# The first microseconds of a graph kernel: whole-float32 hop 0, an earlier input wait, split biases, and weights laid out in 2 KB runs

## What is computed

```python
Xw = X @ Wv + bv
sj, si = Xw @ aw[:d, 0], Xw @ aw[d:, 0]
e = leaky_relu(sj[:, None, :] + si[:, :, None] + ab[0], 0.2)
alpha = A * exp(e)
T = alpha / (sum(alpha, axis=-1, keepdims=True) + 1e-12)
H, Xk = 0, X
for k in range(3):                  # hops 0, 1, 2
    H = H + Xk @ Wk[k] + bk[k]
    Xk = einsum('bij,bjd->bid', T, Xk)
x = layernorm(x + relu(H))
x = layernorm(x + (adj @ x) @ w)
```

## Time and profile before

| | us |
|---|---|
| median of 3 executions | 272.84 (272.76 to 273.21) |
| the profiled execution | 273.95 |
| its span | 272.1 |
| TensorE busy | 266.3 (98%) |
| VectorE busy | 216.8 (80%) |
| ScalarE busy | 191.6 (70%) |
| GpSimd busy | 190.3 (70%) |

### The profile page before, as it was taken

One profiled execution on the slowest core, in us unless ns is written; L12 is line 12 of the kernel. 1 busy time (PEld: TensorE's weight loads), 2 busy tenths in 40 slices (PEclk: granted clock), 3 DMA queues, 4 the chain that ended last, 5 costly groups with the idle time before them and its releaser, 6 DMA issues.

```text
span 272.1 us, 6029 instructions
## 1 busy us (share of the span) xinstructions
PE 266.3 (98%) x1887; PEld 246.6 (91%) x1887; DVE 216.8 (80%) x615; ACT 191.6 (70%) x437; POOL 190.3 (70%) x412
## 2 busy tenths in 40 slices
PE   8999999999999999999999999999999999999992
PEld 3899999999999999999999999999999999999991
DVE  0677788888898888889888888988888888788994
ACT  2688677776667777666777766677766677767874
POOL 2567547788777777877778787777887777657533
PEclk9999999999999999999999999999999999999998
DMA  7858245749584378545764448844883347922214
GB/s 222 292 164 135 30 147 125 81 139 150 150 151 145 58 136 140 165 142 155 126 86 123 146 155 143 150 121 79 133 161 99 117 115 87 135 75 77 79 41 154
DMA packets 28758, 34.91 MB, mean 128 GB/s; under 512 B 7091, under 2 KB 16694, under 8 KB 28726
## 3 DMA queue, kind: packets, MB, share of 16 engines
q1 hardware_dynamic: 28016, 34.12, 56.7%
q10 hardware_dynamic: 710, 0.40, 0.5%
HBM read 26.09 MB, written 8.42 MB: 127 GB/s over the span
## 4 chain that ended last, share of the span: by engine, by line
PE 93%; DVE 2%; DMA 1%; POOL 1%; ACT 1%; issue 1%; POOLq 0%; ACTq 0%
PE ps_v L1123 30%; PE ps_y L1123 16%; PE ps_out L1123 14%; PE ps_h L1123 11%; PE ps_agg L1300 10%; PE ps_v L1233 3%; PE ps_v L1237 3%; PE ps_v L1235 3%; PE ps_agg L1123 2%; DMA WY_sb<-Wk_dram 1%; PE ps_y L1151 1%; PE ps_v L1151 1%; POOL rstd L1025 1%; DVE stats L865 0%; DVE y L878 0%
## 5 line engine op out<-in xcount | busy, mean ns | idle before, releaser
L1123 PE MATMUL ps_v<-WX_hi,XT_hi 128*128 128x512 f32 (+1 forms) x128 | 47.7, 373 | 0.0
L1123 PE MATMUL ps_v<-WX_lo,XT_hi 128*128 128x512 f32 (+1 forms) x128 | 47.4, 371 | 0.0
L1123 PE MATMUL ps_v<-WX_hi,XT_lo 128*128 128x512 f32 (+1 forms) x128 | 47.4, 371 | 0.0
L1040 POOL TENSOR_TENSOR XT_lo<-xt,XT_hi 128x512 fp32r<-128x512 f32 x32 | 41.3, 1293 | 5.4 <-DVE WX_lo L964 2.7
L1052 POOL TENSOR_TENSOR alpha<-exps,adjs 128x256 f32<-128x256 f32 x31 | 22.9, 740 | 30.3 <-ACT exps L477 30.0
L1056 POOL TENSOR_TENSOR alpha_lo<-alpha,alpha_hi 128x256 fp32r<-128x256 f32 x31 | 22.8, 734 | 18.4 <-ACT alpha_hi L486 18.4
L509 ACT ACTIVATE y<-res,offset,rstd 128x256 f32<-128x256 f32 x62 | 33.6, 590 | 0.8 <-POOL offset L1016 0.8
L1123 PE MATMUL ps_y<-WY_hi,XT_hi 128*128 128x258 f32 x112 | 34.1, 304 | 0.0
L1300 PEld LDWEIGHTS ps_agg<-adjs,y 128*128 128x128 f32 x248 | 32.0, 191 | 2.3
L1300 PE MATMUL ps_agg<-adjs,y 128*128 128x128 f32 x248 | 32.7, 275 | 0.0
L502 ACT ACTIVATE V_hi<-ps_v 128x512 fp32r<-128x512 f32 x32 | 19.1, 597 | 19.1 <-PE ps_v L1123 18.9
(11 more groups left out here) (177 smaller groups left out, 838.7 us busy)
## 6 DMA issues: line engine op xcount, KB each, us to landing
xt<-xt_dram SPq DMA_DIRECT2D x32, 256.0 KB, 5.3
nodes<-nodes_dram SPq DMA_DIRECT2D x32, 256.0 KB, 5.4
out_dram<-out_sb SPq DMA_DIRECT2D x30, 256.0 KB, 5.0
adjs<-adjs_dram SPq DMA_DIRECT2D x32, 128.0 KB, 5.3
spread<-si_rows_dram SPq DMA_DIRECT2D x29, 128.0 KB, 4.7
W_sb<-Wk_dram SPq DMA_DIRECT2D x2, 256.0 KB, 3.9
si_rows_dram<-scores SPq DMA_DIRECT2D x29, 1.0 KB, 3.6
WY_sb<-Wk_dram ACTq DMA_DIRECT2D x1, 256.0 KB, 4.1
```

The lines of the kernel that those rows point to most:

```text
L1040: pool.tensor_tensor(XT_lo[k % 7][:].rearrange("p c b i -> p (c b i)"), xt_sb[k % 4][:], XT_hi[k % 7][:].rearrange("p c b i -> p (c b i)") ...
L1123: last = pe.matmul(to, a, b, start=start and n == 0, stop=stop and n == 2, skip_group_check=True)
```

## The change

1. Pair 0 starts with hop 0 in whole float32 (`first_hop0` on TensorE, into `ps_h`, from `xt0` and the new first load W0); its hops 2 and 1 are now in split form. The bias is added to hop 0 later (`first_hop0` on VectorE, behind `first_v`), so nothing waits for X0 ahead of the propagation. `keep_warm` has seven matmuls in place of nine. `hop1` copies out in two halves (`first_half_done`, then `v1_done`).
2. The biases are summed by two fp32r products of `bk_hi` and `bk_lo`, after pair 1's hop 2, into `ps_y`.
3. The first exponentials and alphas lie in PSUM (`ps_out`), so pair 1's need not wait for them. GpSimd makes `XT_lo` 0 first of all, and 1 to 4 before `alphas(1)`, with no wait for `WX_ready[1]`.
4. In step 0 the low half of pair 2's alphas comes ahead of the norm on GpSimd, its high half ahead of `v2_hi(4)` on ScalarE, and `inverse(1)` ahead of `first_h` on VectorE. At the end the last root comes ahead of the normalisation.
5. Weights are laid out on the host so that a partition's part is one run of 2 KB. ScalarE issues W0, then loads its table by a dummy exponential, then issues `bk` and `ab`; the other weights and `vectors` are SyncE's. w is loaded later.

The core of the diff:

```diff
 def load_Wk(n):
-    to = (W0_sb, W1_sb)[n]
-    sp.dma_start(to[:, :, 0:D], Wk[n].rearrange("(c p) n -> p c n", p=P)).then_inc(Wk_loaded[n], DMA)
+    to = (W0_sb, W1_sb, WY_sb)[n]
+    sp.dma_start(to[:].rearrange("p c n -> p (c n)"), Wk[n]).then_inc(Wk_loaded[n], DMA)
...
 # VectorE, start
+dve.wait_ge(WY_hi_ready, 1)
+dve.tensor_tensor(WY_lo[:, :, 0:D], WY_sb[:], WY_hi[:, :, 0:D].bitcast(F32), ALU.subtract)
 dve.wait_ge(u_done, 1)
-dve.tensor_copy(W1_sb[:, :, D:D + 2], ps_u).then_inc(u_ready, 1)
-dve.tensor_copy(WY_sb[:, :, D:D + 2], ps_u).then_inc(u_ready, 1)
-dve.wait_ge(u_ready, 2)
-dve.tensor_copy(WY_hi[:], WY_sb[:]).then_inc(WY_hi_ready, 1)
-dve.tensor_tensor(WY_lo[:], WY_sb[:], WY_hi[:].bitcast(F32), ALU.subtract).then_inc(WY_ready, 1)
+dve.tensor_copy(WY_hi[:, :, D:D + 2], ps_u).then_inc(u_ready, 1)
+dve.wait_ge(u_ready, 1)
+dve.tensor_tensor(WY_lo[:, :, D:D + 2], ps_u, WY_hi[:, :, D:D + 2].bitcast(F32),
+                  ALU.subtract).then_inc(WY_ready, 1)
...
 # VectorE, step(k)
-if k == 0:
-    first_h()
-elif not both_hops(k):
+if k > 0 and not both_hops(k):
     scale_h(k)
 inverse(k + 1)
+if k == 0:
+    first_h()
...
 # ScalarE, prologue
 xt_hi(0)
 wx_hi(0)
+wy_hi()
+wx_hi(1)
+bk_hi_of()
+xt_hi(1)
+xt_hi(2)
+scores_of(0)
 v2_hi(0)
-xt_hi(1)
-first_scores()
-xt_hi(2)
 leaky_of(0)
 exponentials(0)
 xt_hi(3)
 alpha_hi_of(0)
...
 # GpSimd, step(k)
 alphas(k + 2)
+alpha_lo_of(k + 2)
 if k == 0:
     norm1(0)
-alpha_lo_of(k + 2)
...
 # TensorE, prologue
-keep_warm(ps_v[:, 0], 9)
-first_hop2(0)
+keep_warm(ps_v[:, 0], 7)
+first_hop0(0)
 score_weights()
-first_hop2(1)
+first_hop0(1)
+score_shift()
+hop2_and_scores(0)
 first_hop1(0)
-score_shift()
-first_hop1(1)
-sum_of_biases()
 pe.wait_ge(identity_ready, 1)
 spread_scores(0)
-hop0(0)
+first_hop1(1)
 hop2_and_scores(1)
+sum_of_biases()
 pe.wait_ge(ones_columns_ready, 1)
 propagate_v2(0)
...
 # host
+def by_partition(m):
+    return np.ascontiguousarray(m.reshape(m.shape[:-2] + (d // P, P, d)).swapaxes(-3, -2).reshape(m.shape[:-2] + (P, -1)))
```

More of the change, by code:

```diff
@@ L378, in _ @@
             load_adjs(1)
-            sp.dma_start(w_sb[:], w.rearrange("(c p) n -> p c n", p=P)).then_inc(w_loaded, DMA)
+            load_xt(4)
             load_adjs(2)
@@ L396, in step @@
                     load_adjs(k + 3)
-                if there(k + 9) and k >= -5:
+                if there(k + 9) and k >= -4:
                     load_xt(k + 9)
@@ L400, in step @@
                     load_adjs(4)
+                    sp.dma_start(w_sb[:].rearrange("p c n -> p (c n)"), w).then_inc(w_loaded, DMA)
                 if there(k - 3):
                     store(k - 3)
-            for k in range(-5, LAST + 2):
+            for k in range(-4, LAST + 2):
                 step(k)
@@ L632, in _ @@
             alpha_hi_of(0)
[L633 to L636 removed]
             scores_of(1)
[L638 removed]
+            v2_hi(1)
+            xt_hi(4)
             leaky_of(1)
@@ L1141, in hop2_and_scores, with first_hop0 @@
                                        (WY_hi[:, c], WY_lo[:, c]), c == 0, c == C - 1)
-                    if k == 1 and b == 0:
-                        last.then_inc(second_y_half_done, 1)
                 if b == PER - 1:
                     last.then_inc(y_done, 1)
-            def first_product(to, weights, b):
+            def first_hop0(b):
+                pe.wait_ge(xt_loaded[0], DMA)
+                pe.wait_ge(Wk_loaded[0], DMA)
                 X = xt_sb[0][:].rearrange("p (c b i) -> p c b i", c=C, b=PER)
                 for c in range(C):
-                    last = pe.matmul(to, X[:, c, b], weights[:, c], start=c == 0, stop=c == C - 1,
+                    last = pe.matmul(ps_h[:, b], X[:, c, b], W0_sb[:, c], start=b == 0 and c == 0, stop=c == C - 1,
                                      skip_group_check=True)
-                return last
-            def first_hop2(b):
-                pe.wait_ge(xt_loaded[0], DMA)
-                pe.wait_ge(Wk_loaded[2], DMA)
-                last = first_product(ps_y[:, b, 0:D], WY_sb[:, :, 0:D], b)
                 if b == PER - 1:
-                    last.then_inc(y_done, 1)
+                    last.then_inc(h_done, 1)
             def first_hop1(b):
-                pe.wait_ge(Wk_loaded[1], DMA)
-                pe.wait_ge(u_ready, 1)
-                last = first_product(ps_v[:, b, 0:D + 2], W1_sb, b)
-                if b == PER - 1:
-                    last.then_inc(v1_done, 1)
+                pe.wait_ge(WX_ready[1], 1)
+                for c in range(C):
+                    last = product(ps_v[:, b, 0:D], (XT_hi[0][:, c, b], XT_lo[0][:, c, b]),
+                                   (WX_hi[:, c, 0], WX_lo[:, c, 0]), c == 0, c == C - 1)
+                last.then_inc(first_half_done if b == 0 else v1_done, 1)
             def hop1(k):
-                if k == 1:
-                    pe.wait_ge(WX_ready[1], 1)
                 for b in range(PER):
```

168 lines of the change are left out of this document (76 added, 92 removed).

## The result

| | before | after |
|---|---|---|
| median, executions side by side | 273.0 (9, 272.76 to 273.6) | 275.39 (9, 272.66 to 276.32) |
| ratio of the times, 95% interval | | 1.0071 (1.0049 to 1.0092) |
| profiled execution, its span | 273.95, 272.1 | 275.39, 273.6 |

The changed kernel is slower, by about 2.4 us between the medians and about 0.7% by the ratio. Its executions also lie much further apart: two of nine end at or under the upper end of before (272.66 and 273.19), seven at 274.4 or later. The ratios in this document leave out the executions more than 1.5% above the fastest of their kernel (three of e2, three of e8, one of e3), while the medians and ranges hold them all.

A forecast was written before the change was run, and what follows sets the result against it. TensorE, busy 98% of the span, was taken as the bound. Terms 0.4 + 0.12 + 0.19 - 0.1 - 0.05 + 0.1 = 0.66 us off 272.84 gave 272.2 us, with a range of 271.4 to 273.3.

The forecast's parts named there:

- I take 6.5 for W2 (bounds 6.0 and 6.9): Prologue loads: W2, fourth on SyncE's queue, lands at 6.5 us, and TensorE starts pair 0's hop 2 at about 8.5.
- a later `WY_ready`: Pair 0's hop 2 waits for W2's split products; lateness costs its own time, with 0.2 us of slack free.
- The slower rival: Start of TensorE: the clock rises to 2.4 GHz later; a rise at 10 us costs 1.45, giving 273.6 us; chance 16%.
- the idle piece is short: Start of TensorE: argument against a late clock rise, since it idles only from 3.9 to 4.55 us.
- the split took what was said: Behind W2's landing, ahead of hop 2: a high half of 0.63 us and a low half of 0.69.
- The path from the spread scores to TensorE: Pair 0's first alphas: scores spread at 10.66 us, low half done at 13.8, TensorE on at 14.05, 0.4 earlier than before.
- to wait 0.8 us at its end: Before pair 0's propagation: TensorE has done its other work by 13.25 us and waits 0.8 for the alphas.
- The small terms: Alphas of pair 0 to wide products of pair 2: gains 0.12 and 0.19 us, charges 0.1 and 0.05.
- The 0.1 at the end: Last pair: with the root ahead, VectorE's 0.33 us of idling goes; 0.1 gained, bounds 0 and 0.33.
- the sum said 0.66: Whole kernel: all gains and charges together make it 0.66 us faster, 272.84 to 272.2.
- The first group's early start: Pair 0's hop 0: equal 2 KB runs land W0 at 4.45 us, so TensorE starts at 4.55, 0.4 earlier.
- The rival built on this rule: Prologue loads: 1 KB runs lose nothing, so weights land no earlier, W0 at 4.8; 272.6 to 272.8 us; chance 19%, shared.

The follow-up runs named there:

- e2: The changed kernel with six extra constant matmuls ahead of pair 0's hop 2, to fill the wait for W2; median 276.71 us, ratio to before 1.0069.
- e8: The kernel before the change with seven constant matmuls in place of nine; median 273.25 us, ratio to before 1.0017.
- e3: e1 with all weights in the old layout, two runs of 1 KB a partition; median 274.39 us, ratio to before 1.0025.
- e6: e5 with nine constant matmuls ahead of the first group in place of seven; median 272.56 us, ratio to before 0.9988.
- e11: e7 with W1 and the second input issued only once W0 has landed; median 273.21 us, ratio to before 1.0001.
- e13: e6 with W1 and the second input issued only once W0 has landed; median 272.49 us, ratio to before 0.997.
- e16: The changed kernel, still with seven constants, with W1 and the second input issued only once W0 has landed; median 273.25 us, ratio to before 0.9994.
- e7: The changed kernel with nine constant matmuls in place of seven and nothing else; median 273.57 us, ratio to before 1.0021.
- e1: The changed kernel with the load of vectors issued by ScalarE behind W0, no longer by SyncE ahead of W2; median 272.68 us, ratio to before 0.9991.
- e5: e1 with pair 0's scores and high half of V2 ahead of XT_hi of pair 2 on ScalarE; median 273.28 us, ratio to before 1.0023.
- e9: e6 with the last pair's old order, norm of graph 0 ahead of the root of graph 1 on VectorE; median 272.83 us, ratio to before 1.0001.
- e10: e9 with the old orders of step 0 as well; median 272.9 us, ratio to before 0.9995.
- e12: e6 with the weights in the old layout, two runs of 1 KB a partition; median 273.18 us, ratio to before 1.0008.
- e15: e13 with SyncE's store of the late half moved behind the first of the two last stores; median 272.27 us, ratio to before 0.9965.
- e14: e13 with the weights in the old layout, two runs of 1 KB a partition; median 272.31 us, ratio to before 0.9973.

## Why the prediction was wrong

| step | forecast | after | e6 |
|---|---|---|---|
| first group starts | 4.55 | 4.40 | 4.55 |
| W2 lands | 6.5 (6.0 to 6.9) | 7.79 | 5.86 |
| hop 2 of pair 0 starts | 8.5 | 9.48 | 7.57 |
| its twelve products | 1.44 | 2.95 | 1.55 |
| scores spread | 10.66 | 13.12 | 9.81 |
| TensorE on with the alphas | 14.05 | 16.24 | 13.11 |
| wide products of pair 2 | 28.1 to 28.3 | 29.98 | 26.81 |
| span | 271.4 | 273.6 | 270.4 |

**The step that failed is "I take 6.5 for W2 (bounds 6.0 and 6.9)".** It was read off W1, which had landed by 6.36 with the same bytes ahead. But W1 had been issued behind two transfers, and SyncE then waited; in the change SyncE issues six transfers in a row, five of them large, and ScalarE one beside them. The bytes ahead of W2 are the same and the transfers in flight are not: by W2's landing at 7.79 the queues had moved 1.62 MB, where W2 and what stands ahead of it are 1.05. One line (e11, e13, e16) mends it. Why the transfers behind W2 get ahead of it in some executions and not in others, and where the lull comes from, stays open, and the vectors' small pieces may have their part in it: with them on SyncE all three profiled executions with the full row (after, e2, e7) were late, with them on ScalarE three were early (e1, e5, e6) and four late (e3, e9, e10, e12).

**A wait was priced without its fall.** The prediction priced a later `WY_ready` as time lost one for one, and the clock's *rise* as the only thing that could go wrong with it. In the profiled execution, and by their mean clocks in two more of the nine, the clock *fell* in the wait for W2 (1.43 us), and that doubled its price: 1.51 us more for the twelve products alone. W2 was 1.29 later than forecast, and the scores were spread 2.46 later.

**The slower rival had the right mechanism for the other four late executions, and too small a price.** It priced a rise at 10 us, at 273.6, with a chance of 16%. e8 isolates it: with two constants fewer, five of eleven executions take 274.6 to 277.1. In e5's profile the products are still 0.21 apart at 12 us. The cost was some 3.5 us (275.9 against the 272.4 of the better executions of e5), not 1.45. The argument against it, "the idle piece is short", is the second step that failed: the idle piece was 0.50 in after, and four of nine executions seem to have risen late.

**The range was too narrow** on its upper side: neither a W2 beyond 6.9 nor a fall of the clock was in it, and of the late rise only the cheaper half.

**What held.** W0 let the first group start at 4.40 (forecast 4.55), the split took what was said, VectorE's `WY_lo` ended the wait. The path from the spread scores to TensorE takes 3.1 us in after (13.12 to 16.24) and 3.3 in e6, forecast 3.4. TensorE, which was to wait 0.8 us at its end, waited some 0.3 (0.35 in e13): its own work up to there was undersized. `XT_lo` 4 and the alphas' low half of pair 2 no longer hold TensorE. The small terms were undersized: from the alphas of pair 0 to the wide products of pair 2 (in the chain) it took 28.90 - 14.47 = 14.43 before, 13.90 after and 13.85 in e6, a gain of 0.53 to 0.58 where the terms made 0.12 + 0.19 - 0.1 - 0.05 = 0.16. Of these 0.30 are the orders of step 0 (e9 against e10). `normalise1(0)` waited 1.42 for GpSimd in after, and TensorE did not stand for it. The 0.1 at the end did not come: VectorE's last statistics start at 267.31 before and 268.61 after, 4.79 and 4.99 from the end of the span. The swap alone is worth nothing (e9); VectorE's last output does start 1.40 behind those statistics in after and 1.80 before, but the row of stores behind it likely takes that back (e15).

**With both faults mended, the forecast gain is still not there.** e11 is the change with both mended and nothing else: 273.21 against 273.19, ratio 1.0001. Its hop 2 starts at 7.79, 0.7 ahead of the forecast, yet its scores are spread at 10.93 and not at 10.66, because ScalarE takes them only behind the high half of pair 2's input, which it could start at 10.00. The prediction had no term for that wait. e13 turns this order too and has `vectors` on ScalarE: 272.49, 0.77 under the 273.26 of the kernel before beside it, where the sum said 0.66. That the two are close is partly luck. Between the profiled executions e13 gains 14.47 - 13.83 = 0.64 up to the alphas (forecast 0.4) and 14.43 - 13.86 = 0.57 from there to pair 2 (forecast 0.16), and it loses 0.3 from there to the end, 243.5 against 243.2 (forecast: a gain of 0.1).

**The first group's early start held, its reason did not.** The forecast had W0 in at 4.45 thanks to equal runs of 2 KB. With runs of 1 KB SyncE's issue behind W0 went out at 4.40 (e3), 4.26 (e12) and 4.36 (e14), and with 2 KB at 4.28 in after and 4.37 in e6. The layout gave no more than 0.1 there, and why W2 landed only at 4.81 in that place in the kernel before stays open. As for the 2 KB runs, the Trainium skill ("DMA: Bandwidth & Descriptors", Specifications) gives 512 B as the smallest transfer at line rate; e13 and e14 agree with it in the time, which is the same for 2 KB and 1 KB, though W2 landed 0.4 apart. The rival built on this rule had the better view of the layout.

## What to carry to other kernels

A landing time is read off a row only with as many transfers in flight as the new program has; "the same bytes ahead" is not enough, and a wait on the one transfer that is needed first, put ahead of those that can come later, is cheap and makes the start steady. Keep TensorE at constants up to its first real work: two constant matmuls that overrun by 0.15 us (4.55 against 4.40) cost less than stopping short, which 25 of 82 executions answered with microseconds more at the low clock, against 1 of 94. Whether the idle time or the smaller number of constants does it was not separated; idle pieces of 0.18 (before) and 0.21 us (e14) behind nine constants did no harm. Price every new wait of TensorE twice, once as time and once as what the clock does behind it. Compare spreads as well as medians, and before explaining a median by one profile, see from the clocks of the other executions whether they are of its kind.
